# A gated MLP with a generated adapter: one engine's share in pieces, the start and the generator's place in the order

## The reference

```python
# layer 0
scale = cond @ norm_w.T + 1.0
ms = jnp.mean(x * x, axis=-1, keepdims=True)
h = x * (scale[:, None, :] * jax.lax.rsqrt(ms + EPS))
u = h @ up_w.T                      # 256 -> 2 x 1024
val, gate = jnp.split(u, 2, axis=-1)
h = val * jax.nn.gelu(gate, approximate=False)
y = act_quant(h) @ weight_quant(down_w).T + x    # 8-bit rows, ternary weights

# layer 1, with weights made for each sequence
dWd = ((h_lang @ Wdd.T + bdd) * 0.1).reshape(B, BN, D)
dWu = ((h_lang @ Wdu.T + bdu) * 0.1).reshape(B, D, BN)
down = relu(einsum('bld,bnd->bln', x, Wd + dWd) + bd)
out = x + einsum('bln,bdn->bld', down, Wu + dWu) + bu
```

## Time and profile before

| | us |
|---|---|
| median of 3 runs | 509.94 (509.14 to 511.0) |
| the profiled execution, its own time | 509.27 |
| its span, first to last instruction | 507.5 |
| PE busy | 464.9 (92%) |
| PEld busy | 261.9 (52%) |
| DVE busy | 393.3 (77%) |
| ACT busy | 366.0 (72%) |
| POOL busy | 234.5 (46%) |
| mean clock granted to TensorE | 0.988 of full |

### The profile page before, as it was taken

One profiled execution on the slowest core, in us unless ns is written; L12 is line 12 of the kernel. 1 busy time (PEld: TensorE's weight loads), 2 busy tenths in 40 slices (PEclk: granted clock), 3 DMA queues, 4 the chain that ended last, 5 costly groups with the idle time before them and its releaser, 6 DMA issues. The chain is left out here.

```text
span 507.5 us, 9824 instructions
## 1 busy us (share of the span) xinstructions
PE 464.9 (92%) x3206; PEld 261.9 (52%) x3206; DVE 393.3 (77%) x832; ACT 366.0 (72%) x632; POOL 234.5 (46%) x569
## 2 busy tenths in 40 slices
PE   1967988898899999999999999999999999999964
PEld 1334554465455555555555555555555455555542
DVE  3589999999999877888777777778776677666772
ACT  5588778977896777777776858777677666767661
POOL 0256525342533346455554656455444334444433
PEclk9989999999999999999999999999999999999996
DMA  8766795588653356456555565545554455453343
GB/s 305 291 118 187 195 199 157 178 216 180 176 160 80 83 107 130 123 141 137 145 118 134 125 157 124 106 125 126 138 122 109 98 126 126 114 126 84 79 97 105
DMA packets 120402, 71.64 MB, mean 141 GB/s; under 512 B 104672, under 2 KB 105376, under 8 KB 118176
## 3 DMA queue, kind: packets, MB, share of 16 engines
q1 hardware_dynamic: 120112, 70.93, 55.4%
q10 hardware_dynamic: 240, 0.08, 0.1%
HBM read 37.44 MB, written 8.39 MB: 90 GB/s over the span
## 5 line engine op out<-in xcount | busy, mean ns | idle before, releaser
L697 PE MATMUL bank<-up_hi,xs_hi 128*128 128x512 f16 x512 | 154.3, 383 | 5.5 <-DVE xs_lo L557 3.3
L697 PE MATMUL bank<-up_lo,xs_hi 128*128 128x512 f16 x512 | 153.8, 382 | 0.0
L697 PE MATMUL bank<-up_hi,xs_lo 128*128 128x512 f16 x512 | 153.7, 382 | 0.0
L418 ACT ACTIVATE gel<-bank,rms 128x512 f32<-128x512 f32 x128 | 87.2, 681 | 75.5 <-PE bank L697 69.4
L578 DVE SCALAR_TENSOR_TENSOR hid<-bank,rms,gel 128x512 f32<-128x512 f32 x128 | 95.3, 745 | 26.8 <-ACT gel L418 26.5
L423 ACT ACTIVATE hid<-hid,amax 128x1024 f32<-128x1024 f32 x64 | 73.3, 1145 | 32.6 <-DVE amax L592 31.8
L353 POOL TENSOR_TENSOR ad_lo<-adapt,ad_hi 128x256 f16<-128x256 f32 x64 | 41.4, 669 | 91.9 <-DVE ad_hi L624 91.9
L697 PEld LDWEIGHTS bank<-up_lo,xs_hi 128*128 128x128 f16 x512 | 50.5, 99 | 61.9 <-issue 2.6
L697 PEld LDWEIGHTS bank<-up_hi,xs_lo 128*128 128x128 f16 x512 | 50.4, 98 | 61.4 <-issue 1.8
L586 DVE TENSOR_REDUCE amax<-hid 128x1 f32<-128x1024 f32 x64 | 78.1, 1220 | 2.2
L335 POOL TENSOR_TENSOR nwt<-nwt 128x2 f32<-128x2 f32 x96 | 21.7, 226 | 107.8 <-DVE nwt L571 102.8
(11 more groups left out here) (65 smaller groups left out, 622.8 us busy)
## 6 DMA issues: line engine op xcount, KB each, us to landing
xT_s<-in_xT SPq DMA_DIRECT2D x32, 256.0 KB, 3.0
xn_s<-in_xn SPq DMA_DIRECT2D x32, 256.0 KB, 3.1
stage<-in_WddT SPq DMA_DIRECT2D x8, 1024.0 KB, 6.4
stage<-in_WduT SPq DMA_DIRECT2D x8, 1024.0 KB, 5.1
out<-out_s SPq DMA_DIRECT2D x32, 256.0 KB, 2.4
adapt<-in_up_wT SPq DMA_DIRECT2D x4, 512.0 KB, 6.6
x<-in_down_wT SPq DMA_DIRECT2D x1, 1024.0 KB, 12.7
qT<-qn SPq DMA_TRANSPOSE x64, 3.1
```

The costliest lines, as they stand in the source:

```text
L418: nc.scalar.activation(gel[:, c], u_gate[c][:], ACT.Gelu, scale=rms[:, t // TPB % XN_SLOTS, t % TPB:t % TPB + 1]).then_inc(gelu_done, 1)
L697: ins = nc.tensor.matmul(dst[:], a[:, t // TPB % 2, k, cols], w[:, c, k, v, :], start=(k == 0 and n == 0), stop=(k == KD - 1 and n == 2))
```

## The change

Three things are edited. POOL subtracts its 1152 columns of a chunk in four instructions of 288 columns (POOL_PIECES), with one semaphore increment behind the last. The whole generator moves one step later: chunk q is split in step q + 1, multiplied at the end of q + 2, evacuated in q + 3, loaded by the same distance ahead, and the adapters of the early sequences follow (NGEN + 4). At the start, the condition and x of sequence 0 are issued ahead of the up weights, the down weights right behind these and ahead of chunk 0; ACT scales x and squares it before it touches the weights, and DVE makes xs_lo and the root's guess ahead of up_lo; PE waits for the low part of the weights only at its second pass; the Abs pass, its matmul and `ternary` come one step earlier, `base_sum` one later.

```diff
--- before.py
+++ after.py
@@ -47,6 +47,7 @@
 GENERATED = 2 * NGEN
 
 POOL_COLS = 1152
+POOL_PIECES = 4
 
 
 U_SCALE = 256.0
@@ -76,7 +77,7 @@
 
     if b >= B - 3:
         return (NT, NT + 2, NT + 3)[b - B + 3]
-    return max(2 * b + 7, NGEN + 3 + (4 * b + 2) // 3)
+    return max(2 * b + 7, NGEN + 4 + (4 * b + 2) // 3)
 
 
 ADAPT = [adapter_step(b) for b in range(B)]
@@ -85,6 +86,11 @@
 def scales(s):
 
     return [b for b in range(1, B) if max(2 * b - 2, 1) == s]
+
+
+def chunk(s, lag):
+
+    return [s - 1 - lag] if 0 <= s - 1 - lag < NGEN else []
 
 
 def sequences(s, lead):
@@ -278,19 +284,19 @@
                 sp.wait_ge(out_done, b + 1)
                 sp.dma_start(out[b], out_s[:, b % OUT_SLOTS]).then_inc(stored[b % OUT_SLOTS], 16)
 
+            sp.dma_start(cond2[0:C, :], condT).then_inc(ld_cond, 16)
+            load_x(0)
             for n in range(NC * KD):
                 sp.dma_start(raw_up[:, n // KD, n % KD], up_wT[:, n // KD, n % KD]).then_inc(ld_up[n], 16)
-                if n == 0:
-                    load_x(0)
+            sp.dma_start(raw_down, down_wT).then_inc(ld_down, 16)
+            load_x(1)
             load_chunk(0)
-            load_x(1)
             for i, (w, b) in enumerate(((WdT, bddT), (WuT, bduT))):
                 sp.dma_start(base[:, i, :], w).then_inc(ld_small, 16)
                 sp.dma_start(bias_raw[:, i, :], b).then_inc(ld_small, 16)
             sp.dma_start(bd_col[:], bd).then_inc(ld_small, 16)
             sp.dma_start(bu_row[:], bu.to_broadcast([P, D])).then_inc(ld_small, 16)
             load_chunk(1)
-            sp.dma_start(raw_down, down_wT).then_inc(ld_down, 16)
             for s in range(END):
                 if s <= NT:
                     for t in split_tiles(s - 1):
@@ -304,8 +310,9 @@
                     store(b)
                 if s % TPB == 0 and s // TPB + 2 < B:
                     load_x(s // TPB + 2)
-                if 2 <= s + 2 < NGEN:
-                    load_chunk(s + 2)
+                for q in chunk(s, -2):
+                    if q >= 2:
+                        load_chunk(q)
 
             sp.wait_ge(turn, 2 * NT)
             for i in range(OUT_SLOTS):
@@ -320,10 +327,13 @@
             nc.gpsimd.memset(ones[:], 1.0).then_inc(const_ready, 1)
 
             def low_part(q):
-                cols = slice(CHUNK - POOL_COLS, CHUNK)
                 pool.wait_ge(w_hi_p, q + 1)
-                nc.gpsimd.tensor_tensor(wsplit[:, q % 2, 1, cols], stage[:, q % 2, cols], wsplit[:, q % 2, 0, cols],
-                                        ALU.subtract).then_inc(w_lo_p, 1)
+                piece = POOL_COLS // POOL_PIECES
+                for i in range(POOL_PIECES):
+                    cols = slice(CHUNK - POOL_COLS + i * piece, CHUNK - POOL_COLS + (i + 1) * piece)
+                    ins = nc.gpsimd.tensor_tensor(wsplit[:, q % 2, 1, cols], stage[:, q % 2, cols],
+                                                  wsplit[:, q % 2, 0, cols], ALU.subtract)
+                ins.then_inc(w_lo_p, 1)
 
             def rsqrt(b):
                 nh, y, tmp = nwt[:, 1], nwt[:, 2], nwt[:, 3]
@@ -376,8 +386,8 @@
                     adapter_low(b)
                 for b in sequences(s, 0):
                     output_bias(b)
-                if s < NGEN:
-                    low_part(s)
+                for q in chunk(s, 0):
+                    low_part(q)
 
         @block.scalar
         def _(act):
@@ -448,24 +458,25 @@
                                          scale=1.0 / A_SCALE).then_inc(relu_done, 1)
 
             act.dma_start(normw[:], norm_wT).then_inc(ld_cond, 16)
-            for half in range(2):
-                act.dma_start(cond2[half * C:(half + 1) * C, :], condT).then_inc(ld_cond, 16)
+            act.dma_start(cond2[C:2 * C, :], condT).then_inc(ld_cond, 16)
             act.wait_ge(const_ready, 2)
             nc.scalar.activation(warm[:], zero[:], ACT.Gelu)
 
+            scaled_high(0)
+            squares(0)
             for n in range(NC * KD):
                 act.wait_ge(ld_up[n], 16)
                 nc.scalar.activation(up_part(up_hi, n // KD, n % KD), raw_up[:, n // KD, n % KD], ACT.Copy, scale=U_SCALE
                                      ).then_inc(up_hi_ready, 1)
-                if n == 0:
-                    scaled_high(0)
-                if n == 1:
-                    squares(0)
             for s in range(END):
                 for b in sequences(s, -1):
                     relu(b)
                 if s < NT:
                     gelu(s, 0)
+                if s == 0:
+                    act.wait_ge(ld_down, 16)
+                    nc.scalar.activation(tern[:].rearrange("p j d -> p (j d)"), raw_down, ACT.Abs,
+                                         accum_out=wsum[:, 0:1]).then_inc(absum_ready, 1)
                 if 0 <= s - 1 < NT:
                     quantize(s - 1)
                 if s < NT:
@@ -480,14 +491,10 @@
                     gelu(s, 1)
                 if s % TPB == 0 and s // TPB + 1 < B:
                     scaled_high(s // TPB + 1)
-                if s < NGEN:
-                    high_part(s)
+                for q in chunk(s, 0):
+                    high_part(q)
                 for b in scales(s + 1):
                     squares(b)
-                if s == 1:
-                    act.wait_ge(ld_down, 16)
-                    nc.scalar.activation(tern[:].rearrange("p j d -> p (j d)"), raw_down, ACT.Abs,
-                                         accum_out=wsum[:, 0:1]).then_inc(absum_ready, 1)
 
         @block.vector
         def _(dve):
@@ -630,19 +637,20 @@
                 nc.vector.scalar_tensor_tensor(out=o, in0=out_ps[b % 2][:], scalar=1.0 / A_SCALE,
                                                in1=o, op0=ALU.mult, op1=ALU.add).then_inc(out_done, 1)
 
+            scaled_low(0)
+            rsqrt_guess(0)
             for n in range(NC * KD):
                 c, k = n // KD, n % KD
                 dve.wait_ge(up_hi_ready, n + 1)
                 nc.vector.scalar_tensor_tensor(out=up_part(up_lo, c, k), in0=raw_up[:, c, k], scalar=U_SCALE,
                                                in1=up_part(up_hi, c, k), op0=ALU.mult, op1=ALU.subtract
                                                ).then_inc(up_ready, 1)
-                if n == 0:
-                    scaled_low(0)
-            rsqrt_guess(0)
             for s in range(END):
                 if s < NT:
                     gate(s, 0)
                 if s == 1:
+                    ternary()
+                if s == 2:
                     base_sum()
                 if 0 <= s - DOWN < NT:
                     dequantization(s - DOWN)
@@ -650,13 +658,11 @@
                 if s < NT:
                     for b in sequences(s, -2):
                         total(b)
-                if 2 <= s < NGEN + 2:
-                    evacuate(s - 2, 0)
-                    evacuate(s - 2, 1)
+                for q in chunk(s, 2):
+                    evacuate(q, 0)
+                    evacuate(q, 1)
                 for b in scales(s):
                     rsqrt_guess(b)
-                if s == 2:
-                    ternary()
                 if s % TPB == 0 and s // TPB + 1 < B:
                     scaled_low(s // TPB + 1)
                 for b in sequences(s, 2):
@@ -689,10 +695,12 @@
                 after(pe, hid_done, (t - 1) * NC + c + 1)
                 cols = slice(t % TPB * P, (t % TPB + 1) * P)
                 for k in range(KD):
-                    if t == 0:
-                        pe.wait_ge(up_ready, c * KD + k + 1)
                     passes = ((xs_hi, up_hi), (xs_hi, up_lo), (xs_lo, up_hi))
                     for n, (a, w) in enumerate(passes):
+                        if t == 0 and n == 0:
+                            pe.wait_ge(up_hi_ready, c * KD + k + 1)
+                        if t == 0 and n == 1:
+                            pe.wait_ge(up_ready, c * KD + k + 1)
                         for v, dst in enumerate((u_val[c], u_gate[c])):
                             ins = nc.tensor.matmul(dst[:], a[:, t // TPB % 2, k, cols], w[:, c, k, v, :],
                                                    start=(k == 0 and n == 0), stop=(k == KD - 1 and n == 2))
@@ -751,7 +759,7 @@
                     if s % TPB == 0:
                         pe.wait_ge(xs_done, s // TPB + 1)
                     up(s, 0)
-                if s == 2:
+                if s == 1:
 
                     pe.wait_ge(const_ready, 5)
                     pe.wait_ge(absum_ready, 1)
@@ -760,8 +768,8 @@
                     down(s - DOWN)
                 if s < NT:
                     up(s, 1)
-                if 1 <= s < NGEN + 1:
-                    generate(s - 1)
+                for q in chunk(s, 1):
+                    generate(q)
                 for b in sequences(s, -1):
                     output(b)
                 for b in sequences(s, 0):
```

## The result

The changed kernel takes 505.59 us (median of 4 runs, 504.99 to 505.92), the kernel before 510.47 (4 runs, 509.14 to 511.49): a ratio of 0.9903, with a 95% interval of 0.988 to 0.9925. It is 4.9 us faster where 12.7 were forecast (509.3 to 496.6), and the time lies outside the range of 490 to 505. The profiled execution's span is 504.1 us.

What follows compares the result with a forecast made beforehand. DVE, standing behind POOL's long instruction, was taken to bound the chunk stage, and PE everything after about 160 us. 509.3 - 8.5 (pieces) - 4.5 (start) + 0.3 (thirteenth step) = 496.6 us, range 490 to 505.

Steps and rivals of the forecast that it cites:

- the pieces: Chunk stage: DVE gets in between POOL's four pieces, a pair of steps falls from 17.20 to 15.78 us, -8.5 us.
- Rival A: Chunk stage: the pieces never let DVE in, so it waits for all four; slower, 514.6 us, chance 0.10.
- Rival C: Chunk stage: DVE waits at xs_lo for ACT's xs_hi instead, a pair stays at 16.8 us; 503 us, chance 0.14.
- The 14.22 us that I called DVE's real work: Chunk stage: DVE's 17.20 us pair less 0.61 idle and 2.37 standing behind POOL, below PE's 15.25.
- This 0.4 us a chunk I put at nothing: POOL in the chunk stage: four pieces take 2.8 us instead of 2.37, covered by POOL's free time; uncovered 6.4 us.
- the +0.3 of the thirteenth full step: End of the chunk stage: the chunk put off at the start is paid as one more full step, +0.3 us.
- Start: First steps: sooner small loads and the generator one step later, -4.5 us; bounds -2 and -6.3.
- my lower bound, PE's gaps costing it the upper clock once more: Steps 1 and 2: small loads no sooner and PE's gaps costing its upper clock once more leave only -2 us.
- Adapters come a step later ... PE's work there is the same: nothing: Early sequences' adapters: one step later, the last three stay, PE's work the same, so no cost.
- behind that PE is full and passes it on: After 160 us: PE is busy 40.00 of 40.00 us, so the gain made before then is kept.
- stage 8.5 forecast: Chunk stage: six pairs from the end of step 3 to that of step 15, each saving 1.42 us, -8.5 us.
- The forecast had the tail unchanged: End of the run: last evacuation about 12 us sooner than today's 167, the tail after it unchanged.

Runs made afterwards that it cites:

- e9: Kernel before with POOL's four pieces, new start, ACT making POOL's high part first, POOL's chunk ahead of the root from step 2: 497.86 us, ratio 0.9746.
- e2: Kernel before with only the early sequences' adapters one step later (NGEN + 4): 515.43 us, ratio 1.0091.
- e3: Changed kernel with the adapters two steps later than at first instead of one (NGEN + 5): 500.23 us, ratio 0.979.

## Why the prediction was wrong

**What bounded the kernel, and the pieces: right.** DVE stood behind POOL's one long instruction, it gets in between pieces in order of arrival, and 15.78 us a pair was forecast for 15.95. Alone, the pieces moved the time by -10.2 us between medians (-9.0 in the profiles by step 18). Rival A fell on line 521's 1.56 us (1.65 at most). Rival C was right in kind and wrong in place: the wait for xs_hi stayed at 0.61, and the new wait is the one below. The 14.22 us that I called DVE's real work holds some 0.5 us of short gaps between its instructions: DVE is busy 16.10 us of a pair, less 2.37 of standing. The gaps are there in the new pair as well, so the sum stands. The rule of the Trainium skill that spoke for A (GPSIMD Engine Reference, 2.1 Instruction dispatch) is not contradicted by this, but what I drew from it is: four pieces with no wait between them do let DVE in; one POOL piece out of a chunk takes up to 1.59 us where the median is 0.73.

**"This 0.4 us a chunk I put at nothing": wrong.** I took that cost as covered because POOL's free time is large in sum, and didn't look at when its chunk ends. In steps with a root POOL comes to its chunk late, and with DVE's 0.9 us in between it ends at 91.99 when PE stands ready at 91.19 (92.08 less its wait of 0.89). That brings DVE the 0.40 us of waiting for the gelu behind PE, which its shorter standing (0.70 a pair for 0.95 forecast) makes up only in part: 0.17 over the forecast, 1.0 in six pairs. The first pair gained less, 0.9 us, with a wait of 1.24 us for POOL's chunk in it. It is also the +0.3 of the thirteenth full step: the last chunk is now multiplied in step 17 with such a wait (1.07 us), and from step 17 to 18 the lead went from 12.35 to 9.40, 1.4 of it the chunk's own matmuls and 1.55 lost for 0.3 forecast. The pair of eight pieces (16.52 us) and that of e9 (15.58), where the wait is all but gone, show the cause.

**Start: half right.** PE's first product began at 9.55 us (10.45 forecast), the first gelu at 15.00 (16.0), since the small loads landed at 3.94, sooner than the better bound I gave:

```profile
3.94 1.06 PE L685 MATMUL bank<-cond,normw 64*128 64x32 f32 x4 [3.94 <-DMA cond<-in_condT]
...
9.55 1.01 PE L705 MATMUL bank<-up_hi,xs_hi 128*128 128x512 f16 x2 [4.56 <-ACT up_hi L469]
...
15.00 0.69 ACT L428 ACTIVATE gel<-bank,rms 128x512 f32<-128x512 f32 x1 [1.43 <-PE bank L705]
```

Late next were the up weights, now behind x: PE waited 4.56 us for the first high part. What the sooner start had over went in steps 1 and 2, where PE waited for the gate behind the ternary and for POOL's first chunk, as drawn up; its waits in the first 45 us of the changed kernel:

```profile
PE bank L705 <- ACT up_hi L469: 4.6, 1, 4.6
PE bank L685 <- DMA cond<-in_condT: 3.9, 1, 3.9
PE bank L705 <- DVE hid L585: 2.6, 2, 2.1
PE bank L729 <- POOL wsplit L334: 2.3, 1, 2.3
```

At step 4 the lead was 5.20 with one chunk open, 3.8 without, for 4.5 forecast.

The 0.7 us that are short lie on PE, and I had carried DVE's list only. DVE was through with step 2 at 40.49 us (41.1 forecast) and then waited 0.91 and 0.93 us in step 3 and 4 for gelus behind PE. PE had no wait from 34.83 us to the end of step 4, but its granted clock was at the lower level up to 38.1, right after its wait of 2.3 us for POOL's first chunk:

```profile
34.00:38.00 4.00, 3.17 (x50) 2.75 (x51) 3.48 (x9) 4.00 (x7) 2.66 (x10) 0.62 0.56 145
```

The chunk and the four up matmuls behind it took 3.85 us to 38.68; at the upper level they take 2.3, so this fall cost about 1.6 us (an estimate from the same matmuls later in the run). An earlier fall, at 28.14 us behind the wait of 2.1, seems hidden: the next gelu waited to 31.5 us for the root, and PE then for POOL's chunk. The kernel before has one fall, at 34.1 us, and DVE, which bounds it there, doesn't wait for PE from 34.6 to 54.0. So my lower bound, PE's gaps costing it the upper clock once more, came true in part. No run has the changed kernel without the fall, so that it makes up just these 0.7 us is not shown.

**"Adapters come a step later ... PE's work there is the same: nothing": the failed step.** It cost 4.5 us, the largest miss. The work was the same, but I had not looked at what stands ahead of it on POOL's list in even and in odd steps: with two of three adapters on even steps, behind the root, mid_lo began 4 us after its relu (254.97 for 251.0), and PE waited 0.44 us in every four steps. And "behind that PE is full and passes it on" held only as long as nothing there moved: a kernel at 40.00 of 40.00 has no room for a 0.44 us wait every four steps. By itself (e2) the edit costs 4.6 us.

Summed against the forecast of -12.7: start 0.7 short, stage 8.5 forecast and 7.15 measured (table, steps 4 to 17), thirteenth step 1.25 short, adapters 4.5 short; -12.7 + 0.7 + 1.35 + 1.25 + 4.5 = -4.9, and the table has -4.94.

## What to carry to other kernels

Where two engines stand in each other's way, split the longer instruction only as far as its own end stays covered: alone in the kernel before, two pieces gained 1.7%, four 2.0% (the two are not clearly apart) and eight 0.7%. A step that is moved in a schedule with a period must be looked at in each phase of that period, on every engine's list; a shift by a whole period (e3) is safe where a shift by half of it (e2) is not. And time the parts of a bundled change alone: here one edit gained 10 us, another gave 5 of them back, and the generator's move, for which the adapters were moved at all, shows no gain.

## What the runs showed of the hardware

PE's granted clock stood at 1.00 from 55 to 480 us in every profile but one. In e2's the up matmuls from 136.13 to 139.5 us stand 0.42 us apart instead of 0.215, the lower level of 1.2 GHz instead of 2.4. It came soon after a wait of 1.44 us, and behind five others like it the clock did not fall; the stretches of that kernel (PEclk is the third number from the end):

```profile
124.00:132.00 8.00, 8.00 (x85) 4.78 (x83) 7.21 (x12) 7.34 (x10) 4.85 (x13) 1.00 0.68 220
132.00:140.00 8.00, 6.04 (x62) 3.05 (x61) 7.44 (x11) 4.74 (x9) 2.42 (x2) 0.79 0.59 164
140.00:148.00 8.00, 8.00 (x85) 4.83 (x84) 5.84 (x12) 6.70 (x9) 2.15 (x11) 1.00 0.76 207
```

It is 1.7 us of that execution (table, e2 at step 17), about the difference between two runs of one kernel.

The changed kernel's lead of 4.94 us at step 65 is 3.4 at the end of its span, and 4.9 between the medians. Its profile takes 19.0 us from there to the end, the one before 17.4, with a clock of 0.50 over its last 8.1 us and 0.73 over the last 7.5 of the one before. The forecast had the tail unchanged; whether the clock alone makes this difference is not shown.
